# Loading the synthesis operands during the mixing, the payload in two parts, and one expert tile less

## The reference, cut to what matters

```
x = x + spectral_conv(ln_c(x))       # spherical harmonics, complex mixing of degrees and orders
t = t + opcode_ffn(ln_t(t))          # integer shifts read from one-hot fields
x = x + spiking_attention(ln_c(x))   # leaky units over 8 steps, 8 heads
t = t + moe(ln_t(t))                 # 8 experts, the best 2 of each token, softmax of the two logits
```

## Time and profile before

| | us |
|---|---|
| median of 3 runs | 1301.36 (1296.43, 1301.36, 1301.63) |
| the profiled execution | 1295.22 |
| its span | 1293.4 |
| PE busy | 993.2 (77% of the span) |
| DVE busy | 859.4 (66%) |
| ACT busy | 654.1 (51%) |
| POOL busy | 564.4 (44%) |

### The profile page before, as it was taken

One profiled execution on the slowest core, in us unless ns is written; L12 is line 12 of the kernel. 1 busy time (PEld: TensorE's weight loads), 2 busy tenths in 40 slices (PEclk: granted clock), 3 DMA queues, 4 the chain that ended last, 5 costly groups with the idle time before them and its releaser, 6 DMA issues. The chain is left out here.

```text
span 1293.4 us, 23831 instructions
## 1 busy us (share of the span) xinstructions
PE 993.2 (77%) x6645; PEld 837.2 (65%) x6646; DVE 859.4 (66%) x2743; ACT 654.1 (51%) x1400; POOL 564.4 (44%) x731
## 2 busy tenths in 40 slices
PE   9847746876677675867666453099999999999997
PEld 7837644654456464746555342088888888888886
DVE  7707633756579898888984765066766766667665
ACT  3427732454868877687755431044444444444443
POOL 3310000121132575656665667535555555555554
PEclk9978977976878978778787655599999999999999
DMA  9997966940010010000000001111111111111110
GB/s 264 227 248 156 240 171 157 271 103 20 20 50 20 20 47 19 30 16 20 25 12 30 22 19 35 60 33 35 42 46 50 48 50 42 46 48 47 49 37 2
DMA packets 111924, 93.12 MB, mean 72 GB/s; under 512 B 8012, under 2 KB 100556, under 8 KB 111081
## 3 DMA queue, kind: packets, MB, share of 16 engines
q1 hardware_dynamic: 83753, 62.28, 20.5%
q0 software_dynamic: 9088, 17.33, 4.1%
q10 hardware_dynamic: 19008, 12.59, 3.8%
HBM read 55.61 MB, written 38.39 MB: 73 GB/s over the span
## 5 line engine op out<-in xcount | busy, mean ns | idle before, releaser
L1721 POOL DMA_INDIRECT out_dram<-res,index x156 | 155.8, 999 | 217.8 <-DVE res L1787 189.8
L1830 ACT ACTIVATE sil<-ps_h 128x512 f32<-128x512 f32 x156 | 93.1, 597 | 254.8 <-PE ps_h L1882 254.8
L1752 DVE TENSOR_TENSOR act_rows<-ps_h,sil 128x512 f32<-128x512 f32 x156 | 108.0, 692 | 133.4 <-ACT sil L1830 133.4
L1901 PE MATMUL ps_y<-r_raw,aT 128*128 x1248 | 164.8, 275 | 0.0
L1901 PEld LDWEIGHTS ps_y<-r_raw,aT 128*128 128x128 f32 x1248 | 151.6, 192 | 0.1
L160 POOL DMA_INDIRECT slots<-x_sb,r_pos x128 | 129.3, 1010 | 47.7 <-issue 36.0
L1880 PE MATMUL ps_h<-r_raw,uTh 128*128 x312 | 137.6, 441 | 1.6 <-DVE uTl L1746 1.6
L1881 PE MATMUL ps_h<-r_raw,uTh 128*128 x312 | 124.7, 400 | 0.0
L1882 PE MATMUL ps_h<-r_raw,uTl 128*128 x312 | 123.0, 394 | 0.0
L1092 PE MATMUL ps_q<-wqkv,zT 128*128 128x256 f32 x256 | 114.1, 537 | 0.0
L1204 POOL TENSOR_TENSOR x_sb<-x_sb,sy 128x256 f32<-128x256 f32 x64 | 43.8, 684 | 137.1 <-ACT sy L1340 136.9
(11 more groups left out here) (242 smaller groups left out, 2468.7 us busy)
## 6 DMA issues: line engine op xcount, KB each, us to landing
slots<-zero SPq DMA_DIRECT2D x4, 2652.0 KB, 23.2
pay<-slots SPq DMA_DIRECT2D x39, 272.0 KB, 2.8
coefc<-coefficients ACTq DMA_DIRECT2D x16, 256.0 KB, 6.2
mixed<-mo ACTq DMA_DIRECT2D x16, 256.0 KB, 9.1
gin<-mixed SPq DMA_DIRECT2D x16, 256.0 KB, 14.7
r_raw<-in_L_ffn_W SPq DMA_DIRECT2D x8, 508.0 KB
out_dram<-res,index POOLq DMA_INDIRECT x156, 2.2
pana<-in_legendre_analysis SPq DMA_DIRECT2D x1, 2048.0 KB, 12.8
```

What stands on the lines that cost most here:

```text
L1721: nc.gpsimd.indirect_dma_start(out_rows, bass.IndirectOffsetOnAxis(at, 0), res[:, m % RES, :], None, bounds_check=TOKENS - 1, oob_is_err=F ...
L1752: nc.vector.tensor_tensor(act_rows[:, k], ps_h[:, k, :, DFF:], sil[:, k], ALU.mult).then_inc(s_act, 1)
L1830: nc.scalar.activation(sil[:, k], ps_h[:, k, :, 0:DFF], ACT.Silu).then_inc(s_sil, 1)
L1901: ins = nc.tensor.matmul(dst, aT[:, k, (2 * e + h) * P:(2 * e + h + 1) * P], raw[:, 4 + h, col], start=(h == 0), stop=(h == 1))
```

## The change

Five things change. The load of `lw` and of `psyn` moves from the start of the synthesis block to SP's queue in the mixing block, behind the last load of `wc`. `gin` becomes a view of the first half of `wc`, whose chunks PE has read once six of the eight are mixed. The 16 loads of `gin` become eight: four, issued when the stores of the first six chunks (24 degrees) have landed, over 24 partitions each with all four quarters of the orders; and four, issued when the last stores have landed, over 8 partitions each, still inside the mixing block. PE waits for all eight before the first synthesis product. In the routing tail, the payload of group NP2 - 2 is cut in two, and its first part with the power goes ahead of `route_deviation`. The experts run over 155 tiles.

```diff
@@ build @@
+        late = ExitStack()
+        mixed, loaded = spectral_conv(nc, t, sb, pb, sem, x_sb, ident, minus_half, x_view, routing, par_rows, s_par, late)
         routing.allocate(sb)
         with ExitStack() as a:
+            weights = synthesis_and_weights(nc, t, sb, pb, sem, ident, minus_half, a, loaded, par_rows, s_par, routing)
+            late.close()
@@ spectral_conv @@
-        wc = sb("wc", [P, WS, O, LW, M], at=both)
+        wc = sb("wc", [P, WS, O, LW, M], at=late, side="right")
...
+            psyn = sb("psyn", [P, M, P], at=late, side="right")
+            lw = sb("lw", [P, 4, C], at=late, side="right")
+            gin = wc[:, 0].rearrange("p o l m -> p (o l m)").rearrange("p (j r m o) -> p j r m o", j=4, r=RB, o=16)
+            s_gin = [sem("mixed_early_degrees_loaded"), sem("mixed_last_degrees_loaded")]
+            EARLY = 6
+
+            def load_mixed(eng, l0, l1, s):
+                for op in range(2):
+                    for half in range(2):
+                        p0 = op * 64 + half * L2
+                        src = mixed[op].rearrange("l (j h r) f -> h l j (r f)", j=4, h=2)[half, l0:l1]
+                        eng.dma_start(gin[p0 + l0:p0 + l1].rearrange("p j r m o -> p j (r m o)"), src).then_inc(s, 16)
...
                     for n in range(WS * LW // LQ, NCH):
                         sp.wait_ge(s_mm, n - WS * LW // LQ + 1)
                         load_late(sp, n)
-
+                    sp.dma_start(lw[:, :, :], t["L1_conv_lin_w"].rearrange("i d c -> d i c")).then_inc(s_load, 16)
+                    sp.dma_start(psyn[:, :, :], t["legendre_synthesis"].rearrange("p (m q) -> p m q", m=M)).then_inc(s_psyn, 16)
+                    sp.wait_ge(s_mm, EARLY)
+                    for k in range(2):
+                        sp.wait_ge(s_mw[k], STORED * EARLY // 2)
+                    load_mixed(sp, 0, EARLY * LQ, s_gin[0])
                     for k in range(2):
                         sp.wait_ge(s_mw[k], STORED * NCH // 2)
+                    load_mixed(sp, EARLY * LQ, L2, s_gin[1])
@@ synthesis_and_weights @@
-                sp.dma_start(lw[:, :, :], t["L1_conv_lin_w"].rearrange("i d c -> d i c")).then_inc(s_load, 16)
-                sp.dma_start(psyn[:, :, :], t["legendre_synthesis"].rearrange("p (m q) -> p m q", m=M)).then_inc(s_psyn, 16)
                 sp.dma_start(einv[:, :], t["fourier_inverse"]).then_inc(s_einv, 16)
-                for j in range(4):
-                    for op in range(2):
-                        for half in range(2):
-                            src = mixed[op].rearrange("l (j h r) f -> j h l (r f)", j=4, h=2)[j, half]
-                            p0 = op * 64 + half * L2
-                            sp.dma_start(gin[p0:p0 + L2, j].rearrange("p r m o -> p (r m o)"), src).then_inc(s_gin[j], 16)
...
                 pe.wait_ge(s_psyn, 16)
+                pe.wait_ge(s_gin[0], 16 * 4)
+                pe.wait_ge(s_gin[1], 16 * 4)
                 for n in range(M):
                     j, at = n // (M // 4), n % (M // 4)
-                    if at == 0:
-                        pe.wait_ge(s_gin[j], 16 * 4)
@@ opcode_and_spikes, GpSimd (pay_power + pay_shares together are the old pay) @@
+        def pay_power(pool, v):
...
+        def pay_shares(pool, v):
...
...
                 add_output(pool, NP2 - 1, LAST)
+                gap_of(pool, NP2 - 2)
+                pay_power(pool, NP2 - 2)
                 route_deviation(pool, NP2 - 1)
-                gap_of(pool, NP2 - 2)
-                pay(pool, NP2 - 2)
+                pay_shares(pool, NP2 - 2)
                 scatter(pool, NP2 - 2, 0, NT)
@@ experts @@
+USED_TILES = NTILES + PAIRS - 1
+    SPARE = SLOT_TILES - USED_TILES
...
                 def turn(i, head=False, last=False):
-                    for m in range(STEPS):
+                    for m in range(STEPS - SPARE if last else STEPS):
...
-                for m in range(3):
-                    scatter(TURNS, m - 3)
+                for m in range(USED_TILES - 3, USED_TILES):
+                    scatter(*divmod(m, STEPS))

```

More of the change, by code:

```diff
@@ L106, in build, with sb @@
     with ExitStack() as ctx:
-        def sb(name, shape, dt=F32, at=ctx):
-            return at.enter_context(nc.sbuf_tensor(name, shape, dt))
+        def sb(name, shape, dt=F32, at=ctx, side=None):
+            return at.enter_context(nc.sbuf_tensor(name, shape, dt, side=side))
         def pb(name, shape, dt=F32, at=ctx):
@@ L201, in inverse_deviation, with spectral_conv @@
     return nc.gpsimd.tensor_tensor(tmp[:, 3, :], tmp[:, 2, :], minus_half[:, 0:tmp.shape[2]], ALU.pow)
-def spectral_conv(nc, t, sb, pb, sem, x_sb, ident, minus_half, x_view, routing, par_rows, s_par):
+def spectral_conv(nc, t, sb, pb, sem, x_sb, ident, minus_half, x_view, routing, par_rows, s_par, late):
     spectral_w = [t["L0_conv_w1r"], t["L0_conv_w1i"], t["L0_conv_w2r"], t["L0_conv_w2i"]]
@@ L550, in _ @@
                         half_mixed(n, 1).then_inc(s_mm, 1)
-    return mixed
+    return mixed, (psyn, lw, gin, s_psyn, s_gin, s_load)
 def split3(nc, chain, parts, x, rest):
@@ L561, in split3, with synthesis_and_weights @@
     return nc.vector.tensor_tensor(parts[2], rest, parts[1], ALU.subtract)
-def synthesis_and_weights(nc, t, sb, pb, sem, ident, minus_half, keep, mixed, par_rows, s_par, routing):
+def synthesis_and_weights(nc, t, sb, pb, sem, ident, minus_half, keep, loaded, par_rows, s_par, routing):
+    psyn, lw, gin, s_psyn, s_gin, s_load = loaded
     wqkv = sb("wqkv", [P, 3 * C], at=keep)
@@ L572, in synthesis_and_weights @@
     with ExitStack() as a:
-        psyn = sb("psyn", [P, M, P], at=a)
-        gin = sb("gin", [P, 4, RB, M // 4, 16], at=a)
         ps_g = pb("ps_g", [P, 2, 2, 256], at=a)
-        s_psyn = sem("c_legendre_loaded")
         s_einv = sem("c_fourier_loaded")
-        s_gin = [sem(f"mixed_loaded_{j}") for j in range(4)]
         s_leg = sem("c_legendre")
         s_h = [sem("c_orders_even"), sem("c_orders_odd")]
-        lw = sb("lw", [P, 4, C], at=a)
         par = sb("par", [P, 5, 4], at=a)
@@ L590, in synthesis_and_weights @@
         ps_p = pb("ps_p", [P, 5 * 4], at=a)
-        s_load = sem("w_loaded")
         s_chain = sem("w_chain")
@@ L1223, in pay @@
             chain.link(nc.gpsimd.tensor_tensor(share[:, 0, :], total[:, :], inverse[:, :], ALU.pow))
+            assert chain.n == POWER_LINKS
+        def pay_shares(pool, v):
+            chain = Chain(pool, s_share, v * SHARE_LINKS + POWER_LINKS)
             chain.link(nc.gpsimd.tensor_tensor(share[:, 1, :], power[:, :], share[:, 0, :], ALU.mult))
@@ L1229, in pay @@
                 .then_inc(s_paid, 1)
-            assert chain.n == SHARE_LINKS
+            assert chain.n == SHARE_LINKS - POWER_LINKS
         def deviation(pool, n):
@@ L1812, in _ @@
                 turn(TURNS - 1, last=True)
-                for m in range(2):
-                    first_part(TURNS, m - 2)
-                    result(TURNS, m - 2)
+                for m in range(USED_TILES - 2, USED_TILES):
+                    first_part(*divmod(m, STEPS))
+                    result(*divmod(m, STEPS))
             @block.scalar
@@ L1851, in _ @@
                 turn(TURNS - 1, last=True)
-                copied(SLOT_TILES - 1, 1)
+                copied(USED_TILES - 1, (USED_TILES - 1) % 2)
             @block.tensor
@@ L1932, in _ @@
                 turn(TURNS - 1, last=True)
-                n = SLOT_TILES
+                n = USED_TILES
                 at_out = [pe.snap(r, min_val=0, max_val=(E - 1) * C) for r in behind]
-                turn_gated(n - 1, 1)
-                expert_out(n - 2, 0, at_out[4:6])
-                expert_out(n - 1, 1, at_out[6:8])
+                turn_gated(n - 1, (n - 1) % 2)
+                for m in (n - 2, n - 1):
+                    q = m % G
+                    expert_out(m, m % 2, at_out[2 * q:2 * q + 2])
 _CONSTANTS = spectral_tables()
```

10 lines of the change are left out of this document (6 added, 4 removed).

## The result

In nine runs of each on one chip the changed kernel took 1305.64 us (median; 1303.61 to 1314.11), the kernel before 1300.12 (1295.94 to 1301.63). The ratio is 1.0069, with a 95% interval from 1.0047 to 1.0091: 6 to 12 us slower, +9 in the middle; the two medians alone differ by 5.5. The profiled execution took 1307.96, with a span of 1306.1 against 1293.4. All ratios here leave out one run of the kernel before that took 3179.54 us, in the comparison of e5 to e7.

What follows compares the result with a forecast made beforehand. Three limits: PE in the experts, POOL in the routing tail, late DMA loads between mixing and synthesis. +13.0 - 1.8 - 2.7 = +8.5 us on the median 1301.36 gave 1309.9 us, range 1296 to 1316.

Steps and rivals of the forecast that it cites:

- rival 3: Mixing to synthesis: last store starves beside gin's 8 KB pieces, lands at 198; +17 instead of +13, 1314 us; chance 0.08.
- Tables at 390 GB/s, nothing of the mixing waits: Mixing: lw and psyn, 2.36 MB, load in 6.0 us from 170, in by 177.5, without delaying the mixing.
- 24 degrees at 169 GB/s, in by 196.1: Early gin loads: 3.15 MB over 24 partitions from 177.5 take 18.6 us.
- Last 8 degrees at 56 GB/s, 18.7 us: Late gin loads: 1.05 MB over 8 partitions, from 196.1 to 214.8; synthesis starts at 215.4.
- each partition keeps its share of it: Narrower gin loads: 7.0 GB/s a partition, so 169 GB/s over 24 partitions and 56 over 8.
- So 187.5 to 193, before the 24 degrees are in: End of mixing: the last store, issued at 183.85, lands within this span, ahead of the early gin loads' end.
- The weights chain is hidden: Before the synthesis: the weights chain ends by 203.5, ahead of the synthesis start at 215.4; costs nothing.
- 21.0 us for the synthesis: Synthesis: its length stays as before once all loads have landed.
- The tail, -1.8: Routing tail: payload moved ahead lets scatters start about 4.8 us earlier; gain 1.8 us, ends 0 and -4.8.
- The tile, -2.7: Experts: one tile less saves 2.7 us of PE's time, ends -2.5 and -2.9.
- The sum: Whole kernel: +13.0 - 1.8 - 2.7 = +8.5 us.
- Rivals 1 and 2: gin loads: 1, rate stays 225 GB/s, 1295 at the middle, chance 0.16; 2, eight engines at 14 GB/s, 1300.5, 0.14.

Runs made afterwards that it cites:

- e5: The kernel before with only the routing tail's payload cut in two parts; 1296.94 us against 1298.95, ratio 0.9984.
- e7: The changed kernel with each load's 8 partitions 4 apart and early gin loads in 512-byte pieces; ratio 1.0003 to the kernel before.
- e3: The changed kernel with each group of 8 degrees on partitions 4 apart instead of side by side; ratio 1.0010 to the kernel before.
- e4: The changed kernel with the 24-degree loads also issued after the last store; 1322.23 us in one run.
- e8: The changed kernel with early gin loads in pieces of 2 KB instead of 8 KB; ratio 1.0077 to the kernel before.
- e10: The changed kernel with each load's 8 partitions 4 apart and early gin loads in 2 KB pieces; ratio 0.9986 to the kernel before.
- e2: The changed kernel with gin loaded as before, late, over 32 partitions and in quarters, tables still during the mixing; 1282.38 us, ratio 0.9899.
- e9: The changed kernel with early gin loads in pieces of 1 KB instead of 8 KB; ratio 1.0085 to the kernel before.
- e6: The changed kernel with early gin loads in pieces of 512 bytes instead of 8 KB; ratio 1.0120 to the kernel before.

## Why the prediction was right or wrong

The forecast of +8.5 us, 1309.9, lies well with the measured +9 (6 to 12) and 1305.64, and the verdict "slower" was right. The base was 1301.36 where the nine runs have 1300.12. One step failed, and that the number came out all the same is partly luck: for a run like the profiled one the prediction said 1303.7, and the profiled execution took 1307.96, 12.7 above the one before, which is what rival 3 asks for (+17 - 1.8 - 2.7 = +12.5). The timed runs are on the whole faster than that one.

- *Tables at 390 GB/s, nothing of the mixing waits*: right (426 from 170 to 175; the last copy and the last store come at the old times).
- *24 degrees at 169 GB/s, in by 196.1*: right (167; the last packets near 197).
- *Last 8 degrees at 56 GB/s, 18.7 us*: right. Their packets run from 201 to about 220.2, 19.2 us, 55 GB/s. e3 confirms the reason given, the receiving side, but my wording was too loose: it isn't "each partition keeps its share of it", it is which partitions.
- *"So 187.5 to 193, before the 24 degrees are in"*: **this step failed.** The store landed near 199. I took its landing from a median over the traffic of the mixing, where no such load ran beside most of them; rival 3 had the mechanism and its numbers (lands at 198, last loads begin at 200), with a chance of only 0.08. e4 shows that the loads beside the store are the cause, e8 to e10 that the share goes by pieces. The store of the seventh chunk, issued at 172.49, had no term of its own at all; it landed at 197.5, and what was left of it stood ahead of the last store in the same queue. So the synthesis started at 220.77 instead of 215.4: 4.9 us from the start of the last loads, 0.5 from their length.
- *The weights chain is hidden*: right, it ended at 211.6, ahead of 220.77. *21.0 us for the synthesis*: right (20.6 to the end of the last copy, 20.9 to the next block).
- *The tail, -1.8*: right in sum (-1.8 in three traces). Its terms: start 5.1 earlier (4.8 predicted), scatters 23.7 us instead of 22.0 (2.2 lost predicted, 1.7 measured), second payload 8.6 instead of 7.0 (0.8 predicted, 1.6 measured).
- *The tile, -2.7*: right (454.4 to 455.0 us in ten traces with 155 tiles against 457.3 and 457.4).
- *The sum*: by the traces +12.7, not +8.5, as the spectral term was 18 instead of 13. The sum of the terms in the trace (offset - 39.8 - 4.7 for tail and tile) fits the timed ratio in e2 (-12.8; measured -13), e3 (+0.6; +1), e9 (+12.0; +11) and e10 (-2.1; -2). It doesn't in e6 (+12.3; +16, interval 14 to 18), e7 (+2.8; 0, interval -1 to 2) and e8 (+13.7; +10, interval 7 to 13), nor in the changed kernel (+13.3; +9, interval 6 to 12). Misses of up to 4 us are as large as the scatter between traces of unchanged code (39.8 and 42.6 in the offset, 535.1 to 540.9 in the stage behind it). So the single traces carry the mechanism, and the timed runs the total.
- *Rivals 1 and 2*: refuted by the changed kernel's own windows (no 225, no 112 GB/s), and e3 shows the same engine share with 203.

## What to carry to other kernels

Ask of a load that is cut to start it earlier which partitions each part covers: eight neighbours took a quarter of the rate of 32. Ask as well whether the consumer can start on one part: e2, with no early start at all, but wide loads cut so that each quarter is enough to begin, beat every version that was cut by degrees. If it must be cut, spread the parts over the partitions. And where small pieces must land while a big load runs on another queue, their share was piece for piece once the turns had begun (loads' pieces of 1 to 8 KB): look at the packets of both queues, not at the bytes, and let nothing important wait on the small ones.

## What the runs showed of the hardware that was not expected

- Two queues on shared engines moved equal numbers of pieces in the stretches from 190 to 194 (88 to 87 with 8 KB against 0.5, 308 to 308 with 2 KB, 576 to 575 with 1 KB). It isn't so everywhere: not in e6 (512 B on both sides), and not in the first us behind an issue. The Trainium skill ("DMA: Bandwidth & Descriptors", "Queues, rings and completion order") says that an engine goes round the queues and drains a packet, typically 9 to 17 descriptors, before it switches. The traces agree with turns of equal length; how many pieces make a turn they don't show, since one for one and nine for nine give the same counts.
- With loads in pieces of 2 KB the last store's pieces stood still for 3 us on the shared engines (five of them against 246), with 1 KB for 4 us (ten against 592). With 8 KB they did not, but there queue 10 had not run empty before.
- With pieces of 512 B the early loads moved about 130 GB/s (e6) and 150 (e7), where pieces of 8 KB moved 167 and 208, and their issue took 2.6 and 1.0 us each, against about 0.7.
- The store's pieces on engines that no load used passed at once: in e3, with the loads on half of the engines, queue 10 moved 617 pieces from 182 to 185, right behind the issue, and then about 30 in a us. Some 90 of the 617 are turns with the loads; the rest is about half of a store's 1,024.
